# Attention slots reordered: scores of the head behind ahead of the older head's weighted sum

## The reference

```python
h = take(weight, token_ids)                       # (8, 512, 256)
x = layernorm(h)
q, k, v = x @ w_aq, x @ w_ak, x @ w_av            # 8 heads of 128
q, k = rope(q), rope(k)
s = q @ k.T / 128 - 1e30 * (i < j)                # causal, 512 x 512 for each head
o = softmax(s) @ v
h = h + o @ w_ao
h = h + experts(layernorm(h))                     # top-1024 tokens for each of 8 experts, gelu
```

## Time and profile before

| | |
|---|---|
| median of 3 runs | 1239.88 us (1239.66 to 1241.63) |
| the profiled execution | 1239.33 us |
| its span, first to last instruction | 1237.4 us |
| busy: TensorE, VectorE, ScalarE, POOL | 1121.4, 830.0, 692.1, 819.0 us |
| mean granted TensorE clock | 0.970 of full |
| attention | up to 748 us of the span |

### The profile page before, as it was taken

One profiled execution on the slowest core, in us unless ns is written; L12 is line 12 of the kernel. 1 busy time (PEld: TensorE's weight loads), 2 busy tenths in 40 slices (PEclk: granted clock), 3 DMA queues, 4 the chain that ended last, 5 costly groups with the idle time before them and its releaser, 6 DMA issues. The chain is left out here.

```text
span 1237.4 us, 19984 instructions
## 1 busy us (share of the span) xinstructions
PE 1121.4 (91%) x6999; PEld 982.0 (79%) x6999; DVE 830.0 (67%) x1964; ACT 692.1 (56%) x1434; POOL 819.0 (66%) x886
## 2 busy tenths in 40 slices
PE   3899999999999999999999998117999999999997
PEld 2788888888888878878888874016999999999996
DVE  4777787887787787887887855774554555554433
ACT  3666666656656666666666654004554654655542
POOL 3797897887887888887987851014664654744534
PEclk9999999999999999999999999558999999999999
DMA  5000110110100100100100003302433523624223
GB/s 191 1 18 1 39 31 1 39 30 2 44 26 1 44 26 1 44 27 3 46 22 35 18 1 108 107 13 57 121 81 67 129 38 101 134 35 108 26 26 34
DMA packets 42211, 58.09 MB, mean 47 GB/s; under 512 B 8897, under 2 KB 34945, under 8 KB 41985
## 3 DMA queue, kind: packets, MB, share of 16 engines
q0 software_dynamic: 13824, 21.24, 9.8%
q1 hardware_dynamic: 28288, 35.58, 8.7%
HBM read 35.71 MB, written 16.91 MB: 43 GB/s over the span
## 5 line engine op out<-in xcount | busy, mean ns | idle before, releaser
L1098 DVE TENSOR_TENSOR hT_lo<-hid,hT_hi 128x512 fp32r<-128x512 f32 x124 | 86.4, 697 | 170.1 <-ACT hT_hi L1245 157.2
L198 POOL TENSOR_SCALAR prob<-prob,row_inv 128x512 f32<-128x512 f32 (+3 forms) x256 | 135.3, 541 | 69.1 <-DVE row_inv L418 67.4
L1242 ACT ACTIVATE hid<-up,b_e 128x512 f32<-128x512 f32 x128 | 88.1, 688 | 150.4 <-PE up L1345 136.1
L272 ACT ACTIVATE prob<-prob,row_min 128x512 f32<-128x512 f32 (+3 forms) x256 | 142.4, 556 | 40.1 <-DVE row_min L411 39.3
L867 POOL DMA_INDIRECT x<-routed_rows,tokens x64 | 84.3, 1318 | 112.7 <-DVE tokens L1092 95.0
L354 DVE TENSOR_TENSOR pT_lo<-bank,pT_hi 128x384 fp32r<-128x384 f32 (+1 forms) x192 | 114.3, 595 | 42.4 <-ACT pT_hi L254 42.4
L878 POOL TENSOR_SCALAR y<-y,gate 128x256 f32<-128x256 f32 x60 | 32.4, 552 | 128.0 <-issue 127.2
L411 DVE CUSTOM_DVE_ANT_0 prob<-bank,mask_row 128x512 f32<-128x512 f32 (+3 forms) x256 | 114.1, 483 | 0.0
L206 POOL TENSOR_TENSOR q_sin<-q_sin,rope_t 128x512 f32<-128x512 f32 x64 | 82.5, 1290 | 43.6 <-ACT q_sin L296 42.0
L887 POOL DMA_INDIRECT out<-y,tokens x60 | 97.2, 1621 | 16.1 <-issue 13.9
L600 PE MATMUL bank<-ident,prob 128*128 128x128 f32 x640 | 101.7, 273 | 5.6 <-POOL prob L198 5.6
(11 more groups left out here) (239 smaller groups left out, 3821.7 us busy)
## 6 DMA issues: line engine op xcount, KB each, us to landing
raw<-in_w SPq DMA_DIRECT2D x16, 1024.0 KB
emb_res<-emb SPq DMA_DIRECT2D x8, 512.0 KB, 3.7
out<-h SPq DMA_DIRECT2D x8, 512.0 KB, 2.9
routed_rows<-x SPq DMA_DIRECT2D x8, 512.0 KB, 3.1
x<-in_wq SPq DMA_DIRECT2D x1, 1024.0 KB, 5.1
x<-in_wk SPq DMA_DIRECT2D x1, 1024.0 KB, 4.9
x<-in_wv SPq DMA_DIRECT2D x1, 1024.0 KB, 7.0
x<-in_wo SPq DMA_DIRECT2D x1, 1024.0 KB, 10.1
```

Source lines behind the costliest of these rows:

```text
L198: nc.gpsimd.tensor_scalar(pr, pr, row_inv[:, h % 2, k:k + 1], 1.0, ALU.mult, ALU.mult).then_inc(s["norm_done"], 1)
L272: nc.scalar.activation(pr, pr, ACT.Exp, bias=row_min[:, h % 2, k:k + 1], scale=-1.0, accum_out=row_sum[:, h % 2, k:k + 1]).then_inc(s["exp ...
L1098: nc.vector.tensor_tensor(out, in_, hi.bitcast(F32), ALU.subtract)\
L1242: nc.scalar.activation(hid[:, t % 2, :], up_ps[t % 2][:], ACT.Gelu, bias=bias)
```

## The change

Four engines' slot orders are rewritten; no instruction is added or taken out.

- TensorE: scores [0] and [1, 2] of head h-1 stand ahead of weigh(h-3) and turn(h-2, 0).
- VectorE: the three minima of those scores stand ahead of o_lo and t_low(h-2, 0). The inverse of rows 0 to 2 moves from the end of the slot to behind v_lo.
- ScalarE: exp 0 stands ahead of q's qk_high, exp 1 behind it, both ahead of o_hi and the first t_high; exp 2 follows that t_high, ahead of v_high. The order was swap, o_hi, t_high 0, q high, exp 0, v_high, k high, exp 1, t_high 1, exp 2, t_high 2, exp 3; it becomes swap, exp 0, q high, exp 1, o_hi, t_high 0, exp 2, v_high, k high, t_high 1, t_high 2, exp 3.
- POOL and SyncE keep their orders.

```diff
@@ ScalarE
                     if live:
                         swap(b, h)
+                    if ok(h - 1):
+                        exp(b, h - 1, 0)
+                    if live:
+                        qk_high(b, h, "q")
+                    if ok(h - 1):
+                        exp(b, h - 1, 1)
                     if ok(h - 3):
                         after(act, "o_done", n - 3 + 1)
                         after(act, "out_done", n - 3)
                         hi_of(oT[0][:], o_ps[:], "o_hi")
                     if ok(h - 2):
                         t_high(b, h - 2, 0)
-                    if live:
-                        qk_high(b, h, "q")
                     if ok(h - 1):
-                        exp(b, h - 1, 0)
+                        exp(b, h - 1, 2)
...
-                    if ok(h - 1):
-                        exp(b, h - 1, 1)
                     if ok(h - 2):
                         t_high(b, h - 2, 1)
-                    if ok(h - 1):
-                        exp(b, h - 1, 2)
-                    if ok(h - 2):
                         t_high(b, h - 2, 2)
@@ VectorE
                     if live:
                         turn_k(b, h)
-                    if ok(h - 3):
-                        after(dve, "o_hi", n - 3 + 1)
-                        low_of(oT[1][:], o_ps[:], oT[0][:], "o_lo")
-                    if ok(h - 2):
-                        t_low(b, h - 2, 0)
                     if ok(h - 1):
                         after(dve, "t_done", 3 * (n - 3) + 3)
                         after(dve, "s_done", 3 * (n - 1) + 1)
...
                         minimum(b, h - 1, 1)
                         minimum(b, h - 1, 2)
+                    if ok(h - 3):
+                        after(dve, "o_hi", n - 3 + 1)
+                        low_of(oT[1][:], o_ps[:], oT[0][:], "o_lo")
+                    if ok(h - 2):
+                        t_low(b, h - 2, 0)
...
                             low_of(v[1][:, t, :], proj_ps[i][:], v[0][:, t, :], "v_lo")
+                    if ok(h - 1):
+                        after(dve, "exp_done", TB * (n - 1) + 3)
+                        inverse(b, h - 1, 0, 3)
...
-                    if ok(h - 1):
-                        after(dve, "exp_done", TB * (n - 1) + 3)
-                        inverse(b, h - 1, 0, 3)
@@ TensorE
                         project(b, h, "k")
-                    if ok(h - 3):
-                        weigh(b, h - 3)
-                    if ok(h - 2):
-                        after(pe, "norm_done", TB * (n - 2) + 2)
-                        turn(b, h - 2, 0)
                     if ok(h - 1):
                         after(pe, "q_lo", n)
                         after(pe, "k_lo", n)
                         after(pe, "s_min", TB * (n - 1))
                         scores(b, h - 1, [0])
                         scores(b, h - 1, [1, 2])
+                    if ok(h - 3):
+                        weigh(b, h - 3)
+                    if ok(h - 2):
+                        after(pe, "norm_done", TB * (n - 2) + 2)
+                        turn(b, h - 2, 0)
```

## The result

The changed kernel takes 1315.05 us in the median of 4 runs (1313.38 to 1319.35) against 1239.91 us (1239.66 to 1241.63): a ratio of 1.0608, 95% interval 1.058 to 1.0636. It is 6.1% slower. The profiled execution took 1315.99 us with a span of 1314.1 us, 76.7 us longer than before.

The account below looks back on a forecast made before the run. TensorE's list of work was taken to bound the kernel, 10.55 us an ordinary slot. Stalls of 64.7 us, less 0.8 in the last slots, plus 9.8 for the clock, made 73.7 on 1239.3: about 1313 us, range 1282 to 1342.

Parts of the forecast that it names:

- slots 1, 2, 4: Ordinary slots: output(h-3, 0) on TensorE stalls 0.99 us and its first matmul is 0.10 longer, 1.09 us each.
- slot 5: Two normalise2 operations on VectorE ahead of v_lo delay the next q: +0.35 to +1.6 us, taken as +0.9.
- slot 6: VectorE comes late out of slot 5, q_cos at 2.65: slot of 12.40 against 10.80 us, +1.60.
- slot 7, without the clock: Normalise holds q_cos to 3.9, output at 11.10: slot of 13.65 against 12.90 us, +0.75, up to +1.9.
- the clock, slots 7 and 0: TensorE's 3.0 us idle in slot 7 lowers the granted clock: 1.4 us, seven times, 9.8 us, ends 0 and 12.
- The chain to the output: From k_cos through minimum 0, exp 0, q high, exp 1, o_hi, o_lo: output at 9.09 where TensorE wants 8.10.
- What was to be hidden was hidden: Work queued behind the waits stays in time: v_lo done at 10.4 before q at 11.64, k_lo 3 us in hand.
- The ends: Batch 0 costs 5.1 us, the last batch 10.3; slots 8 to 10 gain 0.8, ends 0 and -2.2.
- no fast one: Rival: o_lo done by 8.05, so the stall vanishes and the kernel gets faster, 1222 us; chance 0.07.
- half the stall: Rival: ScalarE steps overlap more, 0.5 us a slot instead of 1.09, no clock fall, 1270 us; chance 0.05.
- the clock did not fall in slots 1 to 6: Rival: the clock falls in every slot with a stall, 54 slots at 1.4 us, 1379 us; chance 0.03.
- POOL ended the wait: Rival: POOL's q_sin is late in all slots, output at 9.85 instead of 9.09, 1346 us; chance 0.05.

Follow-up runs that it names:

- e3: Changed kernel with the weighted sum computed twice in slot 7 of every batch, 12 matmuls more on TensorE; 1299.86 us, ratio 1.0479.
- e12: The kernel of e1 with the edits of e3 and e9; 1250.04 us, ratio 1.0085.
- e1: Changed kernel with o_hi moved directly behind exp 0 on ScalarE, ahead of q high and exp 1; 1270.63 us, ratio 1.0243.
- e11: Changed kernel with exp 1 alone moved directly behind o_hi on ScalarE; 1288.52 us, ratio 1.0398.
- e2: Changed kernel with TensorE's order put back, weigh and turn 0 ahead of the scores; 1401.43 us, ratio 1.1295.
- e4: Changed kernel with scores [3] put ahead of the first output product on TensorE; 1302.4 us, ratio 1.0503.
- e9: Kernel before, four normalise2 operations spread singly over slots 4 and 5 on VectorE, POOL's rsqrt2 behind q's add in slot 4; 1235.6 us, ratio 0.9964.
- e7: Kernel before with only normalise2's first two operations moved behind v_lo in slot 5 on VectorE; 1243.33 us, ratio 1.002.

## Why the prediction was right

The forecast was 1313, measured 1315.05. By its steps, in us for a batch (batch 3, before against changed, from the table):

| term | predicted | measured |
|---|---|---|
| slots 1, 2, 4 | 1.09 each | 1.15, 1.16, 1.13 |
| slot 3 | 1.70 | 1.66 |
| slot 5 | 0.9 | 0.37 |
| slot 6 | 1.60 | 0.88 |
| slot 7, without the clock | 0.75 | 0.75 (e3) |
| slot 0, without the clock | 0 | -0.06 |
| the clock, slots 7 and 0 | 1.4 | 2.73 |
| a batch | 9.6 | 9.77 |

**The bound.** TensorE's list sets the stage. e12 shows it from the other side: in batches 1 to 7 no slot without a stall is under 10.5 us, whatever the other engines' order.

**The chain to the output.** Each of its prices held: 5.16 predicted and 5.18 found for minimum 0, 9.09 and 9.11 for the output; in slot 7 q_cos was expected at 3.9 and starts at 3.90, the output 11.10 and 11.05. e1 and e11 shorten it and get back what they shorten; e2 lengthens it at its start and e4 puts work ahead of its end. That the step that overran was on ScalarE, and not the later weigh, is shown by e1 against e2. VectorE's new order was never run by itself.

**What was to be hidden was hidden.** The changed kernel has no wait for k_lo, and v_lo holds TensorE three times only, in batch 0.

**Slots 5 and 6, too dear.** I took two normalise2 operations between 1.1 and 2.8 us. They took 0.73, less than my lower price. VectorE's and POOL's timelines in slot 5, changed kernel:

```profile
379.84 0.73 DVE L450 TENSOR_SCALAR x<-h,mean_var,rstd 128x256 f32<-128x256 f32 x2
380.48 0.68 DVE L353 TENSOR_TENSOR v_lo<-bank,v_hi 128x512 fp32r<-128x512 f32 x1
```

```profile
378.78 1.28 POOL L218 TENSOR_TENSOR qT_lo<-q_cos,qT_hi 128x512 fp32r<-128x512 f32 x1
380.58 1.30 POOL L218 TENSOR_TENSOR kT_lo<-k_cos,kT_hi 128x512 fp32r<-128x512 f32 x1 [0.53 <-ACT kT_hi L254]
```

By its records POOL was done with q's low part 0.22 us after the two began, and then waited for kT_hi. Before, the pair of the earlier trace rows, 434.35 to 437.15, ran beside two POOL instructions without a gap, 434.41 to 437.00:

```profile
434.41 1.29 POOL L212 TENSOR_TENSOR k_cos<-k_cos,k_sin 128x512 f32<-128x512 f32 x1
435.65 1.35 POOL L218 TENSOR_TENSOR qT_lo<-q_cos,qT_hi 128x512 fp32r<-128x512 f32 x1
```

So q_cos was in time in slot 6, 1.68 into it, and the term of 1.60 that rested on its lateness fell to the ordinary one. The 0.37 found in slot 5 is near the lower end of my range, 0.35, by another way than I gave: v_lo was done at 381.16, 0.9 us before the next q, and what set the slot was the output at 9.23, behind a q high that followed POOL's q_cos (376.99) by 0.03 us. The Trainium skill (SBUF — State Buffer, two separate sides) has the later of two such instructions fully blocked until the other is through. The trace agrees: of the pair before, the first ends 0.14 us after k_cos and the second 0.15 us after qT_lo. My step from there to a slot at either end and nothing between does not hold, since one that comes in the middle of POOL's waits for the rest only; the third normalise2 of slot 5 took 0.76 us before and 0.87 in the changed kernel.

**The clock, too cheap.** I took 1.4 us, seven times, from one stretch in batch 0: 9.8 us in all, and e3 gives 15.2. In batch 3 it is 2.14 in slot 7 and 0.59 in slot 0; over the batches 0 in batch 0, 1.6 in batch 1 and 2.7 in each of five. The two errors, 1.25 too much in slots 5 and 6 and 1.3 too little here, cancel in such a batch. That the sum is so near is in part this luck.

**The ends.** Slots 1 to 3 of batch 0 cost 5.0 us (10.76, 11.47, 13.10 against 8.96, 10.85, 10.54) where I had 1.1; the clock was 0.86 between 42 and 66 us there, and 0.97 in e3, whose slots 1 and 3 took 9.55 and 11.69. So 2.6 us are the clock's and 1.15 the ordinary stall of slot 3. The other 1.2 stand beside longer waits: 2.85 us for v_lo at the end of slot 1 (2.36 before), and 0.83 and 0.76 for normalised probabilities and pT_lo in slot 2 (0.59 before). The last slots, from 789.59 to the evacuation's end at 823.98, are 3.4 us longer than before (716.13 to 747.10), predicted 1.75: the gain of 0.8 did not come.

The rivals: no fast one, and not half the stall, since the ordinary idle time is 0.90 us. Outside batch 0 the clock did not fall in slots 1 to 6, whose idle time is 0.9 to 1.45. POOL ended the wait in slot 5, 0.1 us later than the ordinary chain would have; in e4 and e11, whose slots before are shorter, it does so in slot 6 as well.

## What to carry to other kernels

Where an engine's list is as long as the stage, ask of every step moved forward what it is moved in front of, on each engine, and how much reserve that had: here 1.78 us at o_lo against an o_lo that came 2.7 us later. What counts is the sum along the chain: in e1 exp 0 with its wait of 2.3 us still stands ahead of o_hi and costs an ordinary slot nothing, while q high and exp 1 behind it, 1.12 us, overran the reserve. And before moving extra work out of one slot, add up what the next slot's engine already has to do; spreading it one operation to a gap (e9) won 4 us where moving it whole (e7) lost 3.

## What the runs showed of the hardware

The clock can cost more than the stall that lowers it: in slot 7 and the slot behind it 2.73 us, where the later output costs 0.75. An idle time of 0.9 us in every 11.7 left it at 1.00 in the ordinary slots of batches 1 to 7, and so did 1.43 to 1.45 us in slot 3; 1.8 us in every 12.6 (e2) lowered it in four of six ordinary slots; 3.36 us (slot 7) was followed by 4.72 us at 0.50. The length of the idle time alone does not give the price. The same 3.34 to 3.36 us cost nothing in batch 0, 1.6 us in batch 1 and 2.7 in the five others, and in e11, with 3.09 to 3.10 us each time, slot 7 took from 13.40 to 14.95 us. Shortening the idle time to 1.46 us with useless matmuls (e3) was worth 15 us.

The same VectorE operation takes 0.40 to 1.49 us, in three groups: 0.40 to 0.43, 0.76 to 0.87 and 1.38 to 1.49. By line, the 28 normalise2 operations of the kernel before and then of the changed one (minimum/median/maximum ns):

```profile
L451 DVE TENSOR_SCALAR x<-h,mean_var,rstd x28: 400/1069/1492, 166.7 to 706.1; 128x256 f32<-128x256 f32 x28
```

```profile
L450 DVE TENSOR_SCALAR x<-h,mean_var,rstd x28: 403/412/865, 183.1 to 777.7; 128x256 f32<-128x256 f32 x28
```

Nothing of the operation changed. What differs is where it falls beside POOL's work: in slot 5 of batch 4 before, the three longer ones end 0.14 to 0.15 us after a POOL instruction that ran beside them, and the fourth, with POOL's work done, took 0.42.
